# Cross attention of a two-layer decoder: scores made twice, the second time with keys on the partitions, in place of turned probabilities

## What is computed

```python
q = split_heads(query @ Wq + bq)
k = split_heads(bank @ Wk + bk)
v = split_heads(bank @ Wv + bv)
scores = jnp.einsum('bhqd,bhkd->bhqk', q, k) / scale
attn = jax.nn.softmax(scores, axis=-1)
out = jnp.einsum('bhqk,bhkd->bhqd', attn, v)
out = out.transpose(0, 2, 1, 3).reshape(B, -1, D)
return out @ Wo + bo
```

## Time and profile before

| | |
|---|---|
| median of 3 runs | 2616.53 us (2615.01 to 2621.03) |
| profiled execution, span | 2613.8 us |
| TensorE busy | 2432.4 us (93%), 14208 matmuls |
| VectorE, ScalarE, GpSimd busy | 1110.8, 947.7, 585.1 us |
| DMA | 93.60 MB, mean 36 GB/s |
| chain that ended last | PE 86%, DVE 6%, ACT 3%, POOL 3% |

### The profile page before, as it was taken

One profiled execution on the slowest core, in us unless ns is written; L12 is line 12 of the kernel. 1 busy time (PEld: TensorE's weight loads), 2 busy tenths in 40 slices (PEclk: granted clock), 3 DMA queues, 4 the chain that ended last, 5 costly groups with the idle time before them and its releaser, 6 DMA issues.

```text
span 2613.8 us, 38193 instructions
## 1 busy us (share of the span) xinstructions
PE 2432.4 (93%) x14208; PEld 2160.2 (83%) x14208; DVE 1110.8 (42%) x2206; ACT 947.7 (36%) x1892; POOL 585.1 (22%) x397
## 2 busy tenths in 40 slices
PE   4899999999977789699999999998999999999997
PEld 3788888888866667588888888887999999999997
DVE  7455545555457368444556455654640000200022
ACT  2444434454443144343454344533222222311130
POOL 4111101110132634311111011101222222222222
PEclk9899999999978878789999999998999999999998
DMA  3000000000021010100100000000111111111111
GB/s 136 1 24 24 15 8 23 23 23 6 22 81 29 1 44 0 60 1 28 28 27 21 6 27 27 32 1 33 64 48 65 56 64 56 56 56 64 56 57 41
DMA packets 29513, 93.60 MB, mean 36 GB/s; under 512 B 3752, under 2 KB 4008, under 8 KB 29320
## 3 DMA queue, kind: packets, MB, share of 16 engines
q1 hardware_dynamic: 29448, 92.72, 11.0%
HBM read 91.07 MB, written 1.64 MB: 35 GB/s over the span
## 4 chain that ended last, share of the span: by engine, by line
PE 86%; DVE 6%; ACT 3%; POOL 3%; issue 2%; DMA 0%; DVEq 0%; SPq 0%; POOLq 0%; ACTq 0%
PE psS L272 18%; PE psS L274 16%; PE psS L273 16%; PE psT L1337 7%; PE psJ L272 4%; PE psJ L273 4%; PE psJ L274 4%; PE psO L272 4%; PE psO L274 3%; PE psO L273 3%; PE psT L272 2%; PE psT L274 2%; PE psT L273 2%; DVE x_res L884 1%; DVE stats L877 1%
## 5 line engine op out<-in xcount | busy, mean ns | idle before, releaser
L272 PE MATMUL psS<-hid_hi,fw_hi 128*128 128x400 f32 x1152 | 398.1, 346 | 15.4 <-DVE hid_lo L1258 10.6
L274 PE MATMUL psS<-hid_hi,fw_lo 128*128 128x400 f32 x1152 | 400.2, 347 | 0.0
L273 PE MATMUL psS<-hid_lo,fw_hi 128*128 128x400 f32 x1152 | 399.6, 347 | 0.0
L529 POOL TENSOR_TENSOR fw_lo<-raw,fw_hi 128x1024 fp32r<-128x1024 f32 x88 | 216.7, 2464 | 572.1 <-ACT fw_hi L751 572.1
L615 ACT ACTIVATE pT_hi<-psT 128x300 fp32r<-128x300 f32 x512 | 187.4, 418 | 263.0 <-PE psT L1337 262.5
L1258 DVE TENSOR_TENSOR hid_lo<-h_act,hid_hi 128x800 fp32r<-128x800 f32 x32 | 32.3, 1083 | 555.6 <-ACT hid_hi L840 555.6
L606 ACT ACTIVATE p<-psS,nmax 100x722 f32<-100x722 f32 x256 | 221.9, 867 | 68.9 <-DVE nmax L928 36.4
L936 DVE TENSOR_TENSOR pT_lo<-psT,pT_hi 128x300 fp32r<-128x300 f32 x512 | 216.4, 464 | 38.1 <-ACT pT_hi L615 32.8
L370 POOL TENSOR_TENSOR cT_lo<-ctx_raw,cT_hi 128x722 fp32r<-128x722 f32 x58 | 102.1, 1761 | 580.0 <-ACT cT_hi L565 580.0
L272 PEld LDWEIGHTS psS<-hid_hi,fw_hi 128*128 128x128 f32 x1152 | 218.0, 189 | 16.4 <-issue 11.2
L272 PE MATMUL psO<-pT_hi,vv_hi 128*64 128x200 f32 (+1 forms) x768 | 219.2, 285 | 2.4 <-DVE oraw L947 2.4
(11 more groups left out here) (306 smaller groups left out, 4909.4 us busy)
## 6 DMA issues: line engine op xcount, KB each, us to landing
raw<-ffn_dram SPq DMA_DIRECT2D x88, 512.0 KB, 3.2
ctx_raw<-ctxT_dram SPq DMA_DIRECT2D x60, 361.0 KB, 3.1
mask_raw<-mask_dram SPq DMA_DIRECT2D x8, 282.0 KB
raw<-wk_dram SPq DMA_DIRECT2D x4, 512.0 KB, 3.5
raw<-wv_dram SPq DMA_DIRECT2D x4, 512.0 KB, 6.6
raw<-wq_dram SPq DMA_DIRECT2D x4, 512.0 KB, 3.3
raw<-wo_dram SPq DMA_DIRECT2D x4, 512.0 KB, 3.2
cin<-xT_dram SPq DMA_DIRECT2D x1, 1600.0 KB, 8.3
```

The costliest lines, as they stand in the source:

```text
L272: nc.tensor.matmul(out, st[0], mv_[0], start=first, stop=False)
L273: nc.tensor.matmul(out, st[0], mv_[1], start=False, stop=False)
L274: return nc.tensor.matmul(out, st[1], mv_[0], start=False, stop=last)
L529: nc.gpsimd.tensor_tensor(fw.lo[:, e, :], raw[:, e, :], fw.hi[:, e, :], ALU.subtract)\
```

## The change

Scores are made twice. First, for the maximum alone: the three products of hi and lo parts become one matmul whose contraction runs over the three parts stacked on the partitions (`qS` x `kS`, 97 rows with one for the mask), two pieces per head, always into `psS[0]`. VectorE takes the maximum, splits it (`max_parts`), TensorE turns the three parts (`max_turned`, two small transposes per pair) and ScalarE copies them into three further rows of `qS` (`max_rows`). Second, `scores_turned`: six matmuls per head with the keys on the output's partitions (contraction 99 rows, of which three subtract the maximum), 100 columns each. ScalarE makes exp of them twice, in fp32 and rounded (128x600 each), and GpSimd subtracts (`probs_lo`). `weighted` has 6 matmuls of 200 columns per head instead of 9: the values lie as [hi | lo | ones] beside one another, so that one product gives both parts and the sum of the probabilities; VectorE adds the parts up (`heads_out`). The transposes of `p`, of `rinv` and the `sel` matmuls are gone. The inverse sums are four reciprocals of 32x400 on VectorE.

To stack the parts, keys and queries go to DRAM and come back in another layout: `keys_out`, `keys_in`, `queries_out`, `queries_in`, all issued by SP. Values of the next batch and its first scores and keys now interleave behind the last head. Context chunks are made in pairs 3 and 4, two each, the odd ones' lower part by VectorE. The mask's bias is made once. FFN weights load and split behind the attention. Cut to its core:

```diff
@@ SP: keys and queries go out and come back
+            def keys_out(L, b, g, i):
+
+                k0, kn = HALVES[i]
+                wait_apart(sp, A.k_lo, 8 * (NB * L + b) + (2 * g + i + 1))
+                sp.dma_start(k_dram[g % 2, :, :, k0:k0 + kn], kst[:, i, :, 0:kn].bitcast(fp32))\
+                  .then_inc((A.kd_out0, A.kd_out1)[i], 16)
+
+            def keys_in(L, b, g):
+
+                B = b + NB * L
...
+                wait_apart(sp, A.st_mm, H * B + G * (g - 1))
+                for r, x in enumerate((0, 1, 0)):
+                    sp.dma_start(kS[HD * r:HD * (r + 1), g % 2, :, :].bitcast(fp32),
+                                 k_dram[g % 2, :, x, :].rearrange("(j p) n -> p j n", j=G))\
+                      .then_inc((A.ks_in0, A.ks_in1)[g % 2], 16)
...
+                def batch(b, last):
+                    if not last:
+                        context(L, b + 1, (0, 1))
+                    keys_out(L, b, 2, 1)
+                    keys_in(L, b, 2)
+                    if not last:
+                        queries_in(L, b + 1, 0)
+                    keys_out(L, b, 3, 0)
+                    keys_out(L, b, 3, 1)
+                    if not last:
+                        context(L, b + 1, (2, 3))
+                    keys_in(L, b, 3)
...
             attention_loads(0)
-            for n, k in (("u1", 1), ("v1", 2), ("u2", 2), ("v2", 1), ("rq", 2), ("rk", 2), ("rv", 2)):
+            sp.wait_ge(A.o_scaled, NB)
+            for n, k in (("u1", 1), ("v1", 2), ("u2", 2), ("v2", 1), ("rq", 2)):
+                blocks(n, 0, k)
@@ GpSimd
+            def probs_lo(L, b, h):
+
+                wait_apart(pool, A.pt_hi, H * (b + NB * L) + h + 1)
+                nc.gpsimd.tensor_tensor(pT[:, h % 4, :, T:2 * T], p[:, h % 2, :].rearrange("p (k t) -> p k t", k=NKC),
+                                        pT[:, h % 4, :, 0:T], ALU.subtract).then_inc(A.pt_lo, 1)
@@ ScalarE
+                def probs(b, h):
...
+                    nc.scalar.activation(p[:, e, :].rearrange("p (i n) -> p i n", i=2), st_view[e], ACT.Exp,
+                                         scale=SCALE).then_inc(A.exped, 1)
+
                 def probs_hi(b, h):
...
+                    nc.scalar.activation(pT[:, h % 4, :, 0:T].rearrange("p (i k) t -> p i k t", i=2),
+                                         st_view[e].rearrange("p i (k t) -> p i k t", k=HK), ACT.Exp, scale=SCALE)\
+                      .then_inc(A.pt_hi, 1)
+
+                def max_rows(b, t):
+
+                    act.wait_ge(A.t_mm, PAIRS * (b + NB * L) + t + 1)
+                    nc.scalar.activation(qS[STACK:TROWS, 2 * t:2 * t + 2, :],
+                                         psS[0][0:3, KEYS:KEYS + 2 * T].rearrange("p (e t) -> p e t", e=2), ACT.Copy)\
+                      .then_inc(A.rows_set, 1)
@@ VectorE
+                def inverse_sums(b):
+
+                    dve.wait_ge(A.u_done, PAIRS * (b + NB * L) + PAIRS)
+                    for j in range(G):
+                        r = 2 * HD * (1 - j % 2)
+                        rc = nc.vector.reciprocal(rinv[HD * j:HD * (j + 1), :, :], heads_sum[r:r + HD, j:H:G, :])
+                    rc.then_inc(A.r_done, 1)
@@ TensorE
+                    for k0, kn in PIECES:
+                        if k0 and h % 2 == 0:
+                            wait(pe, A.rows_set, PAIRS * B + h // 2)
+                        mm = nc.tensor.matmul(psS[0][0:T, k0:k0 + kn], qS[0:SROWS, h, :],
+                                              kS[0:SROWS, g % 2, j, k0:k0 + kn], start=True, stop=True)
...
+                def scores_turned(b, h):
...
+                    for k in range(NKC):
+                        n = key_rows(k)
+                        k0 = KA * (k // HK) + T * (k % HK)
+                        mm = nc.tensor.matmul(st_bank[h % 2][0:n, k0:k0 + T], kS[0:TROWS, g % 2, j, KC * k:KC * k + n],
+                                              qS[0:TROWS, h, :], start=True, stop=True)
+                    mm.then_inc(A.st_mm, 1)
...
                 def batch(b, last):
+                    for t in range(PAIRS):
+                        if t < PAIRS - 1:
+                            scores(b, 2 * t + 2)
+                        scores_turned(b, 2 * t)
+                        if t >= 1:
+                            weighted(b, 2 * t - 2)
+                        if t < PAIRS - 1:
+                            scores(b, 2 * t + 3)
...
```

More of the change, by code:

```diff
@@ L1067, in _ @@
                 transposed_lo(LN_CONV + b, b)
+            for i in range(2):
+                keys_lo(0, 0, 1, i)
+            queries_lo(0)
             attention(0, LN_ATT0)
@@ L1224, in _ @@
             for j in range(NKC):
-                values_lo(A[1], 0, j)
+                values_lo(1, 0, j)
+            for i in range(2):
+                keys_lo(1, 0, 1, i)
+            queries_lo(1)
             attention(1, LN_ATT1)
@@ L1333, in transposes, with weighted @@
+                def weighted(b, h):
+                    B, t, e = b + NB * L, h // 2, h % 2
+                    pe.wait_ge(A.pt_lo, H * B + h + 1)
+                    if e == 0:
+                        wait(pe, A.u_done, PAIRS * B + t)
                     if h == 0:
@@ L1335, in transposes @@
                     for k in range(NKC):
-                        k0 = KA * (k // HK) + T * (k % HK)
-                        mm = nc.tensor.transpose(psT[:, k0:k0 + T], p[:, h % 2, KC * k:KC * (k + 1)], ident[0:T, 0:T])
-                    mm.then_inc(a.t_mm, 1)
-                def weighted(b, pr, half):
-                    if half == 0:
-                        pe.wait_ge(a.pt_lo, 2 * (H * b + 2 * pr + 2))
-                        wait(pe, a.o_copied, H // 2 * b + pr)
-                    fs = slice(2 * HD * pr, 2 * HD * (pr + 1))
-                    for k in range(HK * half, HK * (half + 1)):
@@ L1375, in batch @@
+                    weighted(b, H - 1)
                     if not last:
-                        values(a, b + 1, 2)
-                    pe.wait_ge(a.rt_copied, b + 1)
-                    for g in range(C):
-                        mm = nc.tensor.matmul(psT[:, g * T:(g + 1) * T], sel[:, g, :], rT[:, :], start=True, stop=True)
-                    mm.then_inc(a.rb_mm, 1)
-                    if not last:
-                        for j in range(3, NKC):
-                            values(a, b + 1, j)
+                        keys(L, b + 1, 1, 1)
+                        scores(b + 1, 0)
+                        values(L, b + 1, 2)
+                        scores(b + 1, 1)
+                        values(L, b + 1, 3)
+                        keys(L, b + 1, 2, 0)
+                        values(L, b + 1, 4)
+                        max_turned(b + 1, 0)
+                        values(L, b + 1, 5)
@@ L1416, in _ @@
                 if b == 0:
-                    pe.wait_ge(A[0].v_lo, NKC)
+                    pe.wait_ge(A.v_lo, NKC)
                 transpose_x(LN_CONV + b, b)
+            for i in range(2):
+                keys(0, 0, 1, i)
             pe.wait_ge(tx_lo, NB)
             pe.wait_ge(w_split, BLOCKS["wq0"] + 2)
-            queries(A[0], wqo)
+            queries(0, wqo)
+            pe.wait_ge(A.q_lo, 2 * C)
+            pe.wait_ge(A.pads, 5)
             attention(0, LN_ATT0)
@@ L1548, in _ @@
             for i in range(2):
[L1549 removed]
+                keys(1, 0, 0, i, weights="wk1")
             for b in range(EARLY, NB):
@@ L1554, in _ @@
             for j in range(NKC):
-                values(A[1], 0, j)
-            pe.wait_ge(A[1].v_lo, NKC)
+                values(1, 0, j)
+            for i in range(2):
+                keys(1, 0, 1, i)
+            pe.wait_ge(A.v_lo, NKC * (NB + 1))
             pe.wait_ge(w_split, BLOCKS["wq1"] + 2)
-            queries(A[1], wqo)
+            queries(1, wqo)
+            pe.wait_ge(A.q_lo, 4 * C)
+            pe.wait_ge(A.pads, 8)
             attention(1, LN_ATT1)
```

754 lines of the change are left out of this document (430 added, 324 removed).

## The result

The changed kernel takes 2749.21 us, median of 4 runs (2744.39 to 2749.89), against 2615.77 before in 4 runs: ratio 1.0496, interval 1.0476 to 1.0516. It is 5% slower, 44 us more than forecast, inside the range. The profiled execution's span is 2747.9 us.

The account below looks back on a forecast made before the run. Attention was taken as bound by TensorE's executed work at its granted clock. Per batch -12.0 + 9.4 + 3.8 + 2.5 = +3.7, times 14 +52; with +2, +17 and +18, +89: 2705 us, range 2500 to 2860 (8 in 10).

Parts of the forecast that it names:

- the two stalls: TensorE waits per batch: for the last key group's load (+9.4 us) and behind the reciprocals at the batch's end (+3.8).
- A: TensorE's own work in an inner batch: fewer score, transpose and weighted passes, sel matmuls gone; -12.0 us per batch.
- Rival 1: Neither stall: reciprocals cost plain work and keys_in comes in time; 2494 us, or 2424 without the clock's fall; chance 0.12.
- rival 2: Slow reciprocals, but key group 3 lands in time in the context pairs; 2564 us, chance 0.18.
- rival 3: Short waits in every pair lower TensorE's mean clock while busy to 0.78; 2873 us, chance 0.12.
- B: Pairs 3 and 4: context chunks on SP's queue delay key group 3, so head 12's scores wait; +9.4 us per batch.
- C: Batch end: four reciprocals of 2.5 us on VectorE delay TensorE's turned maxima and the output projection; +3.8 us per batch.
- D: TensorE's clock: a stall of 9 us in pair 5 adds half of one clock fall; +2.5 us per batch.
- Priced at nothing: In the pairs, GpSimd's 600-element parts can hold up VectorE's operations; VectorE is busy half the time, so no cost charged.
- Starts: Each layer's start: queries through DRAM and back, two-buffer pacing, first keys, scores ahead of the loop; +11.4 us.
- Ends: Behind the last batches, reciprocals without value groups to hide them, +17 us; FFN0's weights loaded and split late, +18.

Follow-up runs that it names:

- the run with neither stall: Changed kernel with one reciprocal after ScalarE gathers the sums, and the last key group's loads issued ahead of context chunks 2 and 3: 2616.5 us, ratio 0.999.
- the run with copies: Changed kernel with its four reciprocals replaced by copies of the same shape: 2657.1 us, ratio 1.015.

## Why the prediction was right, point by point

**The direction and the place.** The forecast was slower by 89 us, with the two stalls as its reasons, and 134 came. Both stalls are in the trace where it put them, and the two runs that take them away bring 41 and 87 to 92 us; together they bring 133, as much as the whole difference: by then A's gain in the loop pays for the starts and for FFN0. Rival 1 (neither stall) and rival 2 (loads in time) are refuted, and so is rival 3 as stated: the clock falls, but to a mean of 0.87 over TensorE's busy time (62.9 of 72.4), not to 0.78. (Its sum had a slip: 67.9 at 0.78 is 87.1 and not 87.5, so 162 us instead of 168.) That the batch came out at 89.4 with 88.7 forecast is in part luck: A was off by 4.6 us one way, the idle time and the clock by 3.2 each the other way.

**A, TensorE's work: -12.0 forecast, -16.6 measured.** The size was off in the favourable direction. A head in TensorE's timeline (columns as in the earlier trace rows):

```profile
326.27 0.33 PE L1510 MATMUL psS<-ident,nmx 100*3 100x100 f32 x2 [1.05 <-DVE nmx L1091]
326.38 0.78 PE L1540 MATMUL psO<-pT,vv 128*96 128x200 f32 x6
327.01 0.57 PE L1502 MATMUL psS<-kS,qS 97*100 97x512 f32 x2
327.42 0.75 PE L1526 MATMUL psS<-qS,kS 99*128 99x100 f32 x6
328.00 0.75 PE L1540 MATMUL psO<-pT,vv 128*96 128x200 f32 x6
328.69 0.57 PE L1502 MATMUL psS<-kS,qS 97*100 97x512 f32 x2
```

From one start to the next: turned maxima of a pair 0.11 and not 0.26, weighted 0.63 and 0.69 (forecast 0.59), two pieces of scores 0.41 with the gap and not 0.50, turned scores 0.58 and not 0.66. I had added a wait to each piece, and a semaphore that is already set shows no time of its own here.

**B, pairs 3 and 4: +9.4 forecast.** The wait was 6.9 us; VectorE's CAST, heads_sum and qS add the rest in these pairs. The mechanism was right (SP's queue), and the landing was 17.4 us behind pair 3's start in the forecast, 347.13 - 327.01 = 20.1 in the trace, of which the three loads took 7.6 where the forecast had 1.2 each. What the forecast had wrong is the worth of the repair: it expected +1.8 without the load's wait, 7.6 less per batch; 2.9 came. The other waits of these pairs were hidden under the load's, and they are each one engine's queue held up by the context of the next batch.

**C, the reciprocals: 2.5 us each forecast, 2.64 measured.** The slope from the row of 16 elements held to 6%. The 3.3 us that the Trainium skill's statement on the iterative divide ("VectorE: DVE Perf Modes", First, the fixed hardware budget) gave as an estimate are too much: 2.64 for 400 elements is 6.6 ns each, not 8.3. The stall was 3.6 us against 2.9.

**D, the clock: +2.5 forecast, +5.7 measured.** Over the five batches 146 us lie at half clock, 29 per batch, where 8 did before: more than one stretch was added. The reason given for this term, the stall of 9 us in pair 5, was wrong: the cost did not go when the wait for the load went (0.865 and 0.866 in those runs), and over five batches of the run with neither stall the clock still adds 8.5 us each, of 9.5. Many brief waits remained there, but that they cause it is not shown: the one run that filled some of them got 1.5 us of clock back. The Trainium skill ("TensorE: Matmul & The Clock Gate", A second HAM failure mode: psum-queue depth-cycling) describes this pattern, a clock that oscillates where TensorE is idle briefly and often between groups; the rows agree as far as they go, 29 us of a batch lie at half clock where TensorE is idle for 19% of it, and rival 3 should have been a term rather than a rival.

**Priced at nothing, and wrong:** GpSimd's parts holding up VectorE. The row of 4.86 us was the warning. VectorE did have slack on average, but the CAST is not average work: TensorE's turned maxima need it in every pair, and in 18 of 40 pairs they had to wait for the parts of the maximum. Over five batches these waits are 27.9 us; about 18 of them are the reciprocals' five stalls of 3.6, which went in the run with copies. The other 10 remained in it; in the batch shown above such waits are 0.27, 1.05 and 0.86 us, behind CASTs that took 1.33, 2.10 and 0.80 longer than their 0.17.

**Starts: +15.1 forecast per layer, first batch included, +34.9 and +28.2 measured.** This is most of the 45 us that were missing: the terms were mis-sized. The chain of layer 0's start, one row of the repeated transfers left out:

```profile
88.74 3.95 DMA k_parts<-kst
...
94.53 7.41 DMA q_parts<-qst
...
103.32 2.51 DMA q_parts<-qst
...
111.10 2.85 DMA q_parts<-qst
...
114.87 1.95 DMA qS<-q_parts
...
123.34 1.99 DVE nmx L1089
125.36 2.27 DVE nmx L1091
...
135.97 4.41 DMA k_parts<-kst
...
141.51 6.62 DMA kS<-k_parts
148.18 0.92 PE psS L1502 x2
```

Queries leave through two buffers, so each pair of halves waits for a transfer and its hand-over: some 3.9 us three times, 11.7 where I had 2. The first of them took 7.4 behind six loads of keys. The two operations on the maximum's parts take 2.0 and 2.3 us, where 0.17 each is their own time. And in the first batch the keys of heads 8 to 11 aren't ahead: 4.4 out and 6.6 in stand in this chain in front of head 8's scores, though TensorE itself waited only 0.5 us for them.

Before, TensorE was at layer 0's first scores at 103 us, now at 117: that is 14 of the 34.9. The other 21 lie behind it, up to the end of the first batch (81.3 us before, 102.5 now). Split by windows of 1 us as above, these are 15.3 less of work, 19.2 more idle and 17.3 more added by the clock, which was granted in full there before and at 0.76 now. In layer 1's first batch the clock adds 7.0 more. So a large part of what the starts' sum lacked is the clock, for which it had 2.5 per batch, and not a load.

**Ends: +17 and +18 forecast.** FFN0's start came out at +18.2. The size was right, the chain only partly: loads and ScalarE's roundings alternate with GpSimd's parts of 2.3 us, and the last link was the load of rq, which alone was worth some 3 us. The last batches were 5.8 and 3.0 us shorter instead of 1.8: A's larger gain without B.

**ScalarE and GpSimd** kept near their prices: 0.67 instead of 0.74 us for an Exp of 600 elements, 1.47 instead of 1.48 for the low part. The context's lower part of 722 columns took 2.38 instead of 1.75, beside a VectorE that now does the other half of it at the same time:

```profile
L487 POOL TENSOR_TENSOR pT<-p,pT 128x600 fp32r<-128x600 f32 x127 | 185.8, 1470 | 383.3 <-ACT pT L742 383.3
L481 POOL TENSOR_TENSOR cT_lo<-ctx_raw,cT_hi 128x722 fp32r<-128x722 f32 x14 | 33.4, 2384 | 0.0
```

## What to carry to other kernels

When an operand gets a round trip through DRAM, look in the queue's order for what stands ahead of its load and what that waits for; a load that is free at its place can hold the critical engine for 7 us per batch behind someone else's wait. An engine whose average is half idle can still hold the critical one in each round, if a tiny operation of it lies on that path: count the queue ahead of the tiny operation, and look whether it ends each time together with another engine's. And removing the longest wait of a stretch brings only the distance to the next one (6.8 us of waiting per batch went, 2.9 us of time came), so price a repair against the second wait and not against zero.

## What the runs showed of the hardware that was not expected

- A reciprocal on VectorE costs the same for 32 partitions (2643 ns) as for 128 (2653 ns), 400 elements each; gathering four quarters first took 87 us off this kernel.
- A CAST of 100x2 elements takes 0.17 us alone and up to 2.27 beside GpSimd, ending 0.02 to 0.03 us after GpSimd's operation does.
- Two subtractions of 128x722 elements that overlap for 0.8 us took 1.66 us on VectorE (L1076) and 2.38 on GpSimd; in the kernel before, without such a one beside it, GpSimd had taken 1.75.
